# Fourier stage: a group's spectrum loaded in four row pieces, its result scattered against the products' count

## What is computed

```python
xn = _layernorm(x, norm1_w, norm1_b)
xf = jnp.fft.rfft2(xn, axes=(1, 2), norm='ortho')            # (8, 32, 17, 192), complex
xf = xf.reshape(B, h, w // 2 + 1, NB, BS)                    # 8 blocks of 24 channels
o1 = jnp.einsum('bhwni,hwnio->bhwno', xf, w1c) + b1c         # own 24 x 24 weights for each (h, w, block)
o1 = complex(relu(o1.real), relu(o1.imag))
xs = jnp.fft.irfft2(o1.reshape(B, h, w // 2 + 1, C), s=(h, w), axes=(1, 2), norm='ortho')
return xs + residual + mlp(_layernorm(xs, norm2_w, norm2_b))
```

## Time and profile before

| | us |
|---|---|
| median of 3 runs | 1142.91 |
| lowest, highest | 1142.13, 1143.01 |
| the profiled execution | 1143.59 |
| span of its trace | 1142.0 |
| products, first start to last end | 69.5 to 254.7 |

### The profile page before, as it was taken

How to read it: one execution, slowest core, us unless ns; L and a number is a source line. 1 busy time by engine, 2 the same in 40 slices (tenths; PEclk the granted TensorE clock), 3 DMA queues, 4 the chain that set the end, 5 groups by cost and what they waited for, 6 DMA issues and landing times. The chain is left out here.

```text
span 1142.0 us, 25847 instructions
## 1 busy us (share of the span) xinstructions
PE 1052.0 (92%) x9224; PEld 809.8 (71%) x9224; DVE 824.8 (72%) x2102; ACT 719.8 (63%) x1325; POOL 345.6 (30%) x365
## 2 busy tenths in 40 slices
PE   4579999986899999997999999999998799999998
PEld 2278888872788888886655655655644588999997
DVE  7565555635788788887697699699699676666665
ACT  4556566646666777665765765765643467666665
POOL 2060112112322222222266176275267011111110
PEclk9888999998899999998999999999998799999999
DMA  9688899957600000001000000000000010111111
GB/s 293 218 176 166 162 182 191 163 125 160 132 1 0 0 0 0 0 0 49 1 1 1 1 1 1 1 1 1 1 1 1 1 28 21 24 25 28 28 28 41
DMA packets 141385, 64.22 MB, mean 56 GB/s; under 512 B 116992, under 2 KB 136096, under 8 KB 141296
## 3 DMA queue, kind: packets, MB, share of 16 engines
q1 hardware_dynamic: 134344, 38.31, 17.6%
q0 software_dynamic: 4096, 11.39, 3.8%
q10 hardware_dynamic: 2864, 13.40, 3.2%
HBM read 44.21 MB, written 12.58 MB: 50 GB/s over the span
## 5 line engine op out<-in xcount | busy, mean ns | idle before, releaser
L1126 PE MATMUL L_conv_ps<-w2hl,L_conv_hhi 128*128 128x384 f32 x768 | 225.7, 362 | 0.0
L934 ACT ACTIVATE L_conv_hf<-L_conv_ps,L_conv_b 128x512 f32<-128x512 f32 x192 | 132.1, 688 | 140.5 <-PE L_conv_ps L1107 139.6
L1126 PE MATMUL L_conv_ps<-w2hl,L_conv_hlo 128*128 128x192 f32 x768 | 187.9, 251 | 0.0
L888 POOL TENSOR_TENSOR X<-X,L_conv_b 128x192 f32 (+1 forms) x128 | 74.6, 614 | 363.9 <-DVE L_conv_hlo L1008 333.0
L1241 POOL TENSOR_TENSOR sc_lo<-XS,sc_hi 128x512 fp32r<-128x512 f32 x96 | 142.6, 1501 | 114.1 <-ACT sc_hi L1317 114.1
L1008 DVE TENSOR_TENSOR L_conv_hlo<-L_conv_hf,L_conv_hhi 128x512 fp32r<-128x512 f32 x192 | 130.2, 692 | 59.1 <-ACT L_conv_hhi L943 58.2
L1126 PEld LDWEIGHTS L_conv_ps<-w2hl,L_conv_hlo 128*128 128x128 f32 x768 | 146.2, 191 | 0.1
L1126 PEld LDWEIGHTS L_conv_ps<-w2hl,L_conv_hhi 128*128 128x128 f32 x768 | 144.4, 188 | 0.1
L1317 ACT ACTIVATE sc_hi<-XS 128x512 fp32r<-128x512 f32 x144 | 87.6, 629 | 81.9 <-DVE XS L1382 27.6
L655 PE MATMUL psF<-spectrum,X 100*24 100x64 f32 x4352 | 128.0, 290 | 8.3 <-issue 4.4
L655 PEld LDWEIGHTS psF<-spectrum,X 100*24 100x24 f32 x4352 | 121.3, 121 | 17.4 <-issue 17.0
(11 more groups left out here) (153 smaller groups left out, 2134.6 us busy)
## 6 DMA issues: line engine op xcount, KB each, us to landing
X<-in_L_conv_w SPq DMA_DIRECT2D x136, 144.0 KB
rows_spectrum<-XS ACTq DMA_DIRECT2D x8, 768.0 KB, 4.7
d<-rows_spectrum ACTq DMA_DIRECT2D x8, 768.0 KB, 4.7
X<-in_x SPq DMA_DIRECT2D x32, 192.0 KB, 4.8
out<-X SPq DMA_DIRECT2D x60, 96.0 KB, 2.3
XS<-d POOLq DMA_DIRECT2D x48, 96.0 KB, 4.5
XS<-in_x POOLq DMA_DIRECT2D x4, 768.0 KB, 9.2
X<-in_x POOLq DMA_DIRECT2D x4, 768.0 KB, 15.7
```

What stands on the lines that cost most here:

```text
L888: nc.gpsimd.tensor_tensor(X[:, GT * i + k, :], X[:, GT * i + k, :], b2[:, :], ALU.add).then_inc(biased if XS is None else based, 1)
L934: nc.scalar.activation(hf[:, m % 3, :], ps[:, RB + m % 2, :], gelu, bias=b1[:, m:m + 1]).then_inc(act1, 1)
L1126: mm = pe.matmul(o, x, w, start=(m == 0 and n == 0), stop=(m == MT - 1 and n == 1), skip_group_check=True)
```

## The change

The load of a group's spectrum, for groups 2 to 7, is cut into four pieces of 32 partitions (192 KB each). Pieces 0 and 1 are issued where the whole was. Piece 2 is issued one unit later, behind `rectify`, piece 3 behind the `spread` that follows. The semaphore counts 16 for each piece, so TensorE's bound in `columns` counts four loads for each earlier group but the first two. On GpSimd each of the eight scatters of groups 0 to 5 gets a wait of its own: scatter `k` waits until the products of unit `last_of[g] + 3` have finished their eighth number `k`.

```diff
                 pool.wait_ge(d3_v, 2 * (g + 1))
                 pool.wait_ge(d3_a, 2 * (g + 1))
                 for k in range(TPB):
+                    pool.wait_ge(mixed, STEP * (last_of[g] + 3) + k + 1)
                     scatter(pool, g, k)
             pool.wait_ge(sh.vectors_in, 16 * n_vectors)
 
@@ -441,8 +442,9 @@
-            def spectrum_rows(g):
-                act.dma_start(d2[g % 2][:, :, :].rearrange("p b c -> p (b c)"), f1_r[g]).then_inc(d2_in[g % 2], 16)
+            def spectrum_rows(g, pieces=None):
+                for rows in [slice(0, P)] if pieces is None else [slice(H * n, H * (n + 1)) for n in pieces]:
+                    act.dma_start(d2[g % 2][rows, :, :].rearrange("p b c -> p (b c)"), f1_r[g][rows]).then_inc(d2_in[g % 2], 16)
 
@@ -482,11 +484,17 @@
             for u in range(UNITS):
                 rectify(u)
+
+                for g in range(NG - 2):
+                    if u + 1 == last_of[g]:
+                        spectrum_rows(g + 2, (2,))
                 if u + 2 < UNITS:
                     spread(u + 2)
                     for g in range(NG - 2):
                         if u + 2 == last_of[g]:
-                            spectrum_rows(g + 2)
+                            spectrum_rows(g + 2, (0, 1))
+                        elif u + 1 == last_of[g]:
+                            spectrum_rows(g + 2, (3,))
@@ -623,7 +631,7 @@
-                pe.wait_ge(d2_in[g % 2], 16 * (g // 2 + 1))
+                pe.wait_ge(d2_in[g % 2], 16 * (4 * (g // 2) + 1))
```

## The result

The change made the kernel slower: 1151.18 us (16 runs, 1145.87 to 1156.27) against 1144.28 us for the kernel before (16 runs, 1141.39 to 1147.57). The ratio is 1.0055 with a 95% interval of 1.0042 to 1.0067, which is +6.3 us, between +4.8 and +7.7. The forecast was 1143.2 us, no measurable change, with a range up to 1146.0. It was wrong.

The account below looks back on a forecast made before the run. TensorE, busy 92% of the span, was taken to bound the kernel, stopping where code blocks come late. Gains of 1.5 us and losses of 1.8 made +0.3, a median of 1143.2 us, range 1140.8 to 1146.0.

Parts of the forecast that it names:

- What bounds the stage, what a gap is, where the change can act: Fourier stage: TensorE bounds; seven gaps inside products, 4.36 us, are late 256-instruction code blocks, all the change could recover.
- an issue sum beyond 7 us: TensorE's issue idle time in the products, 4.4 us before; above 7 us was named as a sign of the collision.
- The base: Median time of the kernel before, taken as 1142.91 us, to which the forecast change was added.
- The scatter's waits, nothing: GpSimd: 48 waits cost 0; only the last two scatters of group 0 find theirs open late, by at most 0.7 us.
- Issues and landing hidden: ScalarE's 18 more issues, 5.9 us of its queue, and the pieces' later landing, with 21 us left, cost 0.
- Gains: Gaps to 92.20, 105.77 and 175.24 us, after loads, shrink with shorter bursts: 1.5 us gained, bounds 0 and 2.14.
- Losses: Half a load on a scatter's tail in four places: 0.9 us at the first, 0.3 at three; 1.8, bounds 0 and 4.8.
- the long block has slack: Code blocks spanning columns and an inverse, some 6.3 us, allow a late fetch; no gap there in three of four places.
- Price of a burst: Half of one load takes nearly all DMA engines for 1.2 us, 0.393 MB at 0.33 MB/us.
- Landing later is covered: Pieces may land later at no cost: 21 us are left before the columns, a whole load takes 4.3 to 5.9.
- The collision: Rival, chance 0.16: load tail, scatter and weights meet in four places, each fetch slips 1.2 us; 1145.6 to 1146.9 us.
- The case that the gaps are not tied to the bursts: Rival, chance 0.05: code fetching is hidden, the seven gaps have a cause DMA order does not touch; 1142.9 us.

Follow-up runs that it names:

- e6: The changed kernel with 32 more small matmuls on TensorE ahead of the first columns; 1.0094 of the kernel before.
- e1: The kernel before with only the scatter's 48 waits on the products added; 0.9992 of the kernel before.
- e3: The kernel before with each load in four pieces of 32 adjacent partitions, all issued in the old place, no scatter waits; 1.0028 of the kernel before.
- e8: The kernel before with each load in four pieces of every fourth partition, all in the old place, no scatter waits; 0.9991 of the kernel before.
- e10: The kernel before with four pieces in the old place, reading 32 adjacent DRAM rows, writing every fourth partition, no scatter waits; 0.9980 of the kernel before.
- e11: The kernel before with four pieces in the old place, reading every fourth DRAM row, writing 32 adjacent partitions, no scatter waits; 1.0030 of the kernel before.
- e2: The changed kernel without the scatter's waits, only the four pieces, two of them one unit later; 1.0051 of the kernel before.
- e9: The whole change, but with each piece on every fourth partition; 1.0010 of the kernel before.
- e13: The changed kernel with the scatters of groups 0 to 5 cut to 16 of 1536 columns; 1140.33 us, 0.9941 of the kernel before.
- e14: The kernel before with the scatters of groups 0 to 5 cut to 16 of 1536 columns; 1140.69 us, 0.9946 of the kernel before.

## Why the prediction was wrong

- **What bounds the stage, what a gap is, where the change can act: right.** Gaps at ends of code blocks (e6), nothing at a unit's first product, 6.5 of the 6.9 us between the two traces inside the stage. The prediction had named an issue sum beyond 7 us as a sign of being wrong; it is 8.4.
- **The base: a small part.** The forecast missed by 8.0 us, 1143.2 against 1151.2. Of that 1.4 lie in the base, 1142.91 in three runs against 1144.28 in sixteen.
- **The scatter's waits, nothing: right.** e1 gave 0.9992; two of 48 waits opened late, by 0.4 us.
- **Issues and landing hidden: right.** The landings took 7.9 us at most, against some 21 us of cover.
- **Gains: right in kind.** The gaps of units 3 and 9 went (0.87 and 0.35). The gap of unit 2 did not: 0.52 + 0.78 for 0.92. 2.14 went and 1.30 came there, 0.84 in sum, forecast 1.5; unit 14 got a new one of 0.37. In unit 2, where 0.3 was to be gained, 0.38 was lost: there all four pieces of group 2 still come together, issued from 84.61 to 90.64 us.
- **Losses: right place, wrong size; this is the step that failed.** The four meetings of half a load with a scatter's tail gave +1.1, +1.75, +1.1 and +0.6 us of gap, 4.5 in sum, where 0.9 + 3 x 0.3 = 1.8 was taken. The reading that "the long block has slack" held in the last three; there it was the next block that failed, and it was charged too little. It was priced from the gaps of 0.22 to 0.46 us that stood there before. Unit 8 had none,

```profile
159.39 7.48 PE L655 MATMUL psF<-spectrum,X 100*24 100x64 f32 x256
```

  but that was no slack: the packet of code for its record 186 ended at 163.24 us, and the record is due at 159.39 + 186 x 0.0289 = 164.77, 1.5 us later, which is just the distance at which gaps end. It was in time by next to nothing.
- **Price of a burst: too low.** Half a load was priced at 1.2 us of all engines from the rate of a whole one. The moved halves held a row for 450 to 484 ns, not 292, so one half is 64 x 470 / 16 = 1.9 us; over all six loads the mean is 426 ns, 46% dearer than the load they replace. "Landing later is covered" answered the wrong question: it is not when the pieces land that counts but how long they hold the engines. The rule on ports quoted above was in no step of it. In time, the adjacent partitions are worth 4 to 5 us where all four pieces stay in the old place (e3 against e8, from two chips; e10 against e11, on one), and the place about 2 (e2 against e3, e9 against e8). The two don't simply add up, as e13 shows.
- **The clock: missing.** +2.4 us of slow columns behind gaps, a term put at nothing. The kernel before had one such row in its timeline, behind the gap of 0.87, and it was passed over:

```profile
108.10 3.46 PE L638 MATMUL psF<-fwd_h,d 128*96 128x128 f32 x16
```

  The gaps were priced by their own length alone, though one can cost up to 1.5 us more in these two traces, if columns stand close behind it.
- **The rivals.** The collision was one of them, with 0.16, at 1145.6 to 1146.9, still below the measured time. Its mechanism is what happened: without the scatter the whole loss is gone (e13 against e14). Its price lacked the slower rows and the clock. The case that the gaps are not tied to the bursts is refuted: they changed with the bursts, and each ends behind a packet of code.

## What to carry to other kernels

A DMA cut along the partitions is not the same load in smaller parts: cut it so that each part still spreads over all partitions, and ask how long it holds the engines, not only when it lands. Long unrolled code is itself a DMA stream; where weights already fill the engines, every further burst that overlaps another one can stop TensorE at the end of a code block, and a stop can cost more than its own length, when wide matmuls follow at the lower clock (0.87 us of gap and 1.47 of slow columns in the kernel before). Before a transfer is moved from one window to another, ask what is already in the other.

## What the runs showed of the hardware

- A row of 6144 bytes into SBUF held a DMA engine, in the mean, for 411 to 417 ns in pieces of 32 adjacent partitions, for 347 ns in pieces of every fourth partition, for 292 ns in one load of 128 (e3, e11; e8, e10; before). The reading side made 6 ns at most.
- The same rows took 450 to 484 ns where they met a scatter, and 292 to 340 ns in the same place without it (after, e13).
- Blocks of code come in 16.4 KB packets, 256 instructions; a gap stands at their ends and moved by 64 records when 128 instructions were put in front (e6). A gap ended 1.28 to 2.11 us behind the end of such a packet (120 gaps, 20 traces). Gaps reached 2.44 us.
- Behind gaps of 1.02 to 1.75 us TensorE's granted clock was 0.50 to 0.61, and 16 column records took 3.21 to 3.45 us instead of 1.99 (after). Behind the gap of 2.22 us it was 0.56 and no columns stood there.
- Cutting six scatters of 768 KB from the kernel before brought 0.54% (e14), though TensorE waited for none of them; the trace places only a sixth of it, as fewer gaps and slow columns.
